# Score products on 64-row tiles in pairs, two products of the second norm on GpSimd, and another order on ScalarE

## The reference, cut to what matters

```
sa, ca, ga, sb, cb, gb = modulation(silu(c) @ wmod)     # per batch, 128 channels each
h = layernorm(x) * (1 + ca) + sa
q, k, v = split(h @ w_attn);  q, k = elu(q) + 1, elu(k) + 1
S_t = S_(t-1) + k_t v_t^T;  z_t = z_(t-1) + k_t         # per head, 8 x 8 state
y_t = (q_t S_t) / (q_t . z_t + 1e-6)
x = x + ga * (y @ w_proj)
h = layernorm(x) * (1 + cb) + sb                        # the second norm
e = argmax(h @ Wg + bg)                                 # one expert per token
x = x + gb * (gelu(h @ W1[e]) @ W2[e])
```

## Time and profile before

| | us |
|---|---|
| median of three runs | 343.55 |
| lowest and highest | 339.87, 344.41 |
| span of the profiled execution | 339.4 |
| stretch of the first 7 steps (about) | 30 to 207 |
| one full step | 24.70 |
| last step, then the tail of routing | 207 to 252 |
| experts | 252 to 339 |

### The profile page before, as it was taken

The page is one execution under the profiler, slowest core; times in us unless marked ns, Lnnn a source line. Parts: engine busy times, 40 slices in busy tenths (PEclk is TensorE's granted clock), DMA queues, the critical chain, the costliest instruction groups (busy, mean ns, idle before and its releaser), DMA issues.

```text
span 339.4 us, 10754 instructions
## 1 busy us (share of the span) xinstructions
PE 285.0 (84%) x3847; PEld 245.5 (72%) x3847; DVE 241.9 (71%) x842; ACT 152.0 (45%) x301; POOL 124.8 (37%) x142
## 2 busy tenths in 40 slices
PE   1777989999999999999999998942129999999980
PEld 1446678688688788787787887742119999999980
DVE  4974557778778778778687787663735888988880
ACT  3378491780871871861952830000023444444430
POOL 8979000303503404305305205232311546545662
PEclk9997999999999999999999999785558999999995
DMA  7990000001000001001001001000252334333410
GB/s 212 319 302 5 3 2 2 2 3 35 34 4 37 27 0 48 16 0 63 1 0 64 0 0 66 2 34 33 82 162 70 108 90 117 93 95 97 113 38 0
DMA packets 16906, 20.19 MB, mean 59 GB/s; under 512 B 2747, under 2 KB 13117, under 8 KB 16882
## 3 DMA queue, kind: packets, MB, share of 16 engines
q1 hardware_dynamic: 13040, 12.50, 13.1%
q0 software_dynamic: 2832, 6.57, 5.6%
q10 hardware_dynamic: 1010, 0.81, 0.8%
HBM read 12.22 MB, written 8.10 MB: 60 GB/s over the span
## 4 chain that ended last, share of the span: by engine, by line
PE 63%; DVE 15%; issue 6%; ACT 4%; POOL 3%; DMA 3%; DVEq 2%; SPq 1%; POOLq 0%; ACTq 0%
PE bank L1001 18%; PE bank L1013 5%; PE bank L1138 5%; PE bank L1147 4%; PE bank L1033 4%; PE bank L1020 4%; PE bank L956 3%; DVE k_q L885 3%; PE bank L1062 3%; PE bank L979 2%; PE bank L971 2%; ACT h_t L432 2%; POOL sorted_rows L374 2%; PE bank L962 2%; PE bank L1047 2%
## 5 line engine op out<-in xcount | busy, mean ns | idle before, releaser
L374 POOL DMA_INDIRECT sorted_rows<-row_buf,slot_i x32 | 31.6, 987 | 119.7 <-DVE slot_i L777 112.4
L1001 PE MATMUL bank<-q_m,k_q 128*64 128x128 f32 x1024 | 71.9, 284 | 2.6 <-DVE probs L654 2.0
L654 DVE TENSOR_TENSOR probs<-bank,causal 128x256 f32<-128x256 f32 x128 | 51.6, 421 | 22.8 <-PE bank L1001 21.9
L1001 PEld LDWEIGHTS bank<-q_m,k_q 128*64 128x64 f32 x1024 | 56.2, 140 | 10.5 <-DVE probs L654 5.9
L396 POOL DMA_INDIRECT out_dram<-q_m,slot_token x39 | 40.8, 1047 | 44.9 <-DVE q_m L901 27.1
L1138 PE MATMUL bank<-q_m,k_q 128*128 128x128 f32 x312 | 43.0, 283 | 0.0
L1147 PE MATMUL bank<-k_q,v_m 128*128 128x128 f32 x312 | 41.5, 276 | 0.0
L1138 PEld LDWEIGHTS bank<-q_m,k_q 128*128 128x128 f32 x312 | 39.6, 199 | 0.0
L1147 PEld LDWEIGHTS bank<-k_q,v_m 128*128 128x128 f32 x312 | 38.1, 193 | 0.4 <-DVE q_m L898 0.4
L541 ACT ACTIVATE v_m<-bank 128x512 f32<-128x512 f32 x39 | 23.3, 598 | 27.2 <-PE bank L1138 27.2
L484 ACT ACTIVATE rden<-bank 128x512 f32<-128x512 f32 x8 | 4.8, 597 | 49.7 <-PE bank L987 49.6
(11 more groups left out here) (177 smaller groups left out, 510.6 us busy)
## 6 DMA issues: line engine op xcount, KB each, us to landing
v_m<-sorted_rows SPq DMA_DIRECT2D x39, 132.0 KB, 2.1
x_all<-in_L_attn_x_dram SPq DMA_DIRECT2D x16, 128.0 KB, 4.2
w_all<-in_L_ffn_W_dram SPq DMA_DIRECT2D x1, 2048.0 KB, 9.6
out_dram<-q_m,slot_token POOLq DMA_INDIRECT x39, 2.3
sorted_rows<-zeros ACTq DMA_DIRECT2D x4, 132.0 KB, 2.3
sorted_rows<-zeros SPq DMA_DIRECT2D x4, 132.0 KB, 2.5
sorted_rows<-row_buf,slot_i POOLq DMA_INDIRECT x32, 2.4
wmod_sb<-in_L_wmod_dram SPq DMA_DIRECT2D x1, 384.0 KB, 4.8
```

The costliest lines, as they stand in the source:

```text
L374: pool.indirect_dma_start(sorted_rows, bass.IndirectOffsetOnAxis(ap=slot_i[par][:, t:t + 1], axis=0), row_buf[par][:, t, :], None).then_in ...
L654: V.tensor_tensor(probs[:, s, b, q, :], score_bank[q % 2][:, 0:QUADS * L], causal[:].rearrange("p a t -> p (a t)"), ALU.mult).then_inc(pro ...
L1001: last = mm(score_bank[q % 2][L * half:L * half + L, 2 * L * n:2 * L * n + 2 * L], k_q[par][:, q, tok:tok + L], q_m[par][:, 2 * half:2 * h ...
```

## The change

`core_scores` now takes two quarters at once. FIRST is (0, 2) and LAST is (1, 3), and `ORDER` gives the new order of quarters. Quarters 0 and 1 live on rows 0 to 63 and go to bank S0, quarters 2 and 3 on rows 64 to 127 and go to S1 (`score_bank[q // 2]`). Each product reads only the 64 rows that hold its quarter; the very first product of a call reads only its 32. The two quarters alternate product by product. One wait, ahead of the call, asks for all quarters before it to be out of their banks. The number of products and of columns is the same.

On POOL, `route_norm` does the product with 1 + cb and the sum with sb as well, each behind a wait for the step before it; `route_modulate` on DVE stays for the last group alone. On ACT, `route_turned` comes before `front_norm`.

```diff
-FIRST, LAST = (0, 1), (2, 3)
+FIRST, LAST = (0, 2), (1, 3)
+ORDER = FIRST + LAST
...
                                         ).then_inc(plain_ready, 1)
+                by_batch = h2.rearrange("p (b s) c -> p b s c", b=B)
+                pool.wait_ge(gates_ready, 1)
+                pool.wait_ge(plain_ready, ready)
+                nc.gpsimd.tensor_tensor(by_batch, by_batch, mod_bc[:, :, 2, :].unsqueeze(2).broadcast_to([P, B, 2, C]),
+                                        ALU.mult).then_inc(scaled, 1)
+                pool.wait_ge(gates_ready, 1)
+                pool.wait_ge(scaled, ready)
+                nc.gpsimd.tensor_tensor(by_batch, by_batch, mod_bc[:, :, 1, :].unsqueeze(2).broadcast_to([P, B, 2, C]),
+                                        ALU.add).then_inc(h2_ready, 1)
...
                     front_kn(f, fpar)
+                if route:
+                    route_turned(g - 1)
                 if norm:
                     front_norm(f + 1)
-                if route:
-                    route_turned(g - 1)
...
                 for q in quads:
-                    dve.wait_ge(score_mm, 16 * g + 8 * s + 4 * b + q + 1)
-                    V.tensor_tensor(probs[:, s, b, q, :], score_bank[q % 2][:, 0:QUADS * L],
+                    dve.wait_ge(score_mm, 16 * g + 8 * s + 4 * b + ORDER.index(q) + 1)
+                    V.tensor_tensor(probs[:, s, b, q, :], score_bank[q // 2][:, 0:QUADS * L],
...
-                if route:
-                    route_modulate(g - 1, 1 - par, chain)
...
-                for q in quads:
-
-                    pe.wait_ge(probs_ready, 16 * g + 8 * s + 4 * b + q + 1)
-                    for n in range(2):
-                        tok = t * P + n * L
-                        for half in range(2):
-                            last = mm(score_bank[q % 2][L * half:L * half + L, 2 * L * n:2 * L * n + 2 * L],
-                                      k_q[par][:, q, tok:tok + L], q_m[par][:, 2 * half:2 * half + 2, tok:tok + L],
-                                      start=True, stop=True)
-                    last.then_inc(score_mm, 1)
+                pe.wait_ge(probs_ready, 16 * g + 8 * s + 4 * b + ORDER.index(quads[1]) + 1)
+                for n in range(2):
+                    tok = t * P + n * L
+                    for half in range(2):
+                        for q in quads:
+                            rows = slice(L * (q // 2), L * (q // 2) + L)
+                            if n == half == 0 and q == quads[0]:
+                                rows = slice(32 * q, 32 * q + 32)
+                            last = mm(score_bank[q // 2][L * half:L * half + L, 2 * L * n:2 * L * n + 2 * L],
+                                      k_q[par][rows, q, tok:tok + L],
+                                      q_m[par][rows, 2 * half:2 * half + 2, tok:tok + L], start=True, stop=True)
+                            if n == 1 and half == 1:
+                                last.then_inc(score_mm, 1)
...
-            core_scores(0, 0, 0, 0)
+            core_scores(0, 0, 0, 0, FIRST)
+            core_scores(0, 0, 0, 0, LAST)
```

More of the change, by code:

```diff
@@ L210, in build @@
         proj_mm, x1_ready = sem("proj_mm"), sem("x1_ready")
-        var2_ready, guess2_ready, norm2_ready, centred, plain_ready = (
-            sem(n) for n in ("var2_ready", "guess2_ready", "norm2_ready", "centred", "plain_ready"))
+        var2_ready, guess2_ready, norm2_ready, centred, plain_ready, scaled = (
+            sem(n) for n in ("var2_ready", "guess2_ready", "norm2_ready", "centred", "plain_ready", "scaled"))
         h2_ready, h2t_mm, h2t_ready, logit_mm, onehot_ready, rank_mm, slots_ready = (
@@ L648, in first_z_and_rden, with core_probs @@
                 rden_and_slots(0, 0, 0, chain, True, False)
-            def core_probs(g, s, b, quads=range(QUADS)):
+            def core_probs(g, s, b, quads=ORDER):
                 wait_ge(dve, y_mm, 4 * g + 2 * s - 1)
                 for q in quads:
-                    dve.wait_ge(score_mm, 16 * g + 8 * s + 4 * b + q + 1)
-                    V.tensor_tensor(probs[:, s, b, q, :], score_bank[q % 2][:, 0:QUADS * L],
+                    dve.wait_ge(score_mm, 16 * g + 8 * s + 4 * b + ORDER.index(q) + 1)
+                    V.tensor_tensor(probs[:, s, b, q, :], score_bank[q // 2][:, 0:QUADS * L],
                                     causal[:].rearrange("p a t -> p (a t)"), ALU.mult).then_inc(probs_ready, 1)
@@ L699, in route_newton, with route_modulate @@
                 newton(rstd2[:], guess2[:], newton2[:], var2[:], chain).then_inc(norm2_ready, 1)
[L701 to L708, removed]
+            def route_modulate(r, par, chain):
+                for t in range(GT):
+                    last = V.tensor_scalar(row_buf[par][:, t, 0:C], row_buf[par][:, t, C:2 * C],
+                                           mean2[:, t:t + 1], rstd2[:, t:t + 1], ALU.subtract, ALU.mult)
+                chain.link(last)
                 h2 = row_buf[par][:, :, 0:C].rearrange("p (b s) c -> p b s c", b=B)
@@ L777, in rden_and_slots @@
                     V.tensor_copy(slot_i[par][:], slot_f[:]).then_inc(slots_ready, 1)
-            LINKS = 3 + 3 + 1 + 7 + 7
+            LINKS = 3 + 3 + 7 + 7
             def step(g, par, turn, chain, front=True, route=True):
@@ L840, in _ @@
             dve.wait_ge(norm2_ready, G)
-            route_modulate(G - 1, 1, chain, norm=True)
+            route_modulate(G - 1, 1, chain)
             z_and_argmax(G, 0, G - 1, chain, False, True)
@@ L988, in front_inv, with core_scores @@
                 last.then_inc(inv_mm, 1)
-            def core_scores(g, par, s, b, quads=range(QUADS)):
+            def core_scores(g, par, s, b, quads):
                 t = 2 * b + s
```

## The result

The changed kernel takes 397.07 us (median of four runs, 392.0 to 398.16) against 343.41 us for the kernel before: a ratio of 1.153, 95% interval 1.138 to 1.169. It is slower, as forecast, but by 53.7 us and not by 10.7, and lies far above the range of 335 to 366. The ratio compares fast runs alone, for the changed kernel the two of 396.25 and 392.0. The profiled execution is the longest of the four, 398.16 us, with a span of 396.4.

The account below looks back on a forecast made before the run. TensorE's own work was taken to bound the step (busy 24.14 of 24.70 us). Five steps +8, the step without xhat +0.6, the first +0.8, opening calls and last step +1.3 gave +10.7: 343.55 to 354 us, range 335 to 366.

Parts of the forecast that it names:

- rival D: TensorE's clock falls in part of the steps after the new waits: another 5 to 20 us, 370, chance 0.05.
- A call of 0.94: One score-product call on TensorE goes from 1.02 to 0.94 us, saving 0.08 a call.
- The lone product's part: Head of a score call: the product alone on 32 rows costs 0.22 for two records plus 0.14 for reshaping.
- the second change of shape: Within a score call, going from 32 to 64 rows costs 0.14, like the loop's changes of column width.
- Rivals A: Score calls: four tiles, first product free, call 0.58, time 335, chance 0.15; beyond 2% faster from below 0.60.
- B: Score calls: second change of shape free, lone product not, call 0.80: +3.4, 347 us, no change, chance 0.17.
- C: Score calls: row halves run one after the other, call 1.38: +34, 377 us, chance 0.08.
- The wait for both banks: Next score call waits until DVE empties both banks: 0.9 us at adjacent calls, 0.3 after the turn.
- ScalarE's order: ScalarE copies h_t before xhat, so q_m comes 4.8 after the turn; TensorE waits 0.95 in five steps.
- GpSimd's products at no cost: Two products moved from DVE to GpSimd, 1.04 each, ready before the turn: cost 0, gain 0.
- A step of 26.3: A full step of the first half, walked once round: 26.3 us, +1.6 on 24.70.
- Rival E: Waits for both banks or q_m don't matter, as freed DVE empties banks earlier: -4, 339 us, chance 0.05.

Follow-up runs that it names:

- e2: The changed kernel with full 128-row score products, no 32- or 64-row product, and ScalarE's order as before: 352.83 us, ratio 1.036.
- e1: The kernel before with score products reading only the 64 rows of their quarter, old order and waits, TensorE's loop written out: 384.53 us, ratio 1.129.
- e11: The kernel before with score products reading only the 32 rows of their quarter, old order and waits, TensorE's loop kept: 389.87 us, ratio 1.091.
- e9: The kernel before with ScalarE's new order alone, e4 again on another chip: 373.26 us, ratio 1.049.
- e10: e9 with five useless 128x128 products on TensorE where it would wait for q_m: 365.41 us, ratio 1.023.
- e4: The kernel before with ScalarE's new order alone (turned rows copied before xhat): median 367.75 us, runs 359.91 to 374.94.
- e3: The changed kernel with ScalarE's order undone (xhat again before the copy of the turned rows): 385.96 us, ratio 1.132.
- e5: The changed kernel without the lone 32-row product, ScalarE's order as before, TensorE's loop written out: 369.74 us, ratio 1.028.
- e6: The kernel before with GpSimd's two products alone, scores and ScalarE's order as before: 360.35 us, ratio 1.000.

## Why the prediction was wrong

**The step that failed is the clock (rival D).** The prediction gave it a chance of 0.05 and 5 to 20 us, and left it out of its sum of 10.7. It was in fact the main case, and with it the loss is 53.7 us: in a full step 6.1 us are lost, of which 1.7 lie in the part at full clock and 4.4 in the rest, where the prediction's own price for waits is 0.2; and up to step 1 another 13 us, of which e2, with the waits but 128 rows, has 5.4. The argument was that PE would still be busy near 90% of a step, and it was: 28.2 of 30.8. That share was the wrong thing to look at. e1 has PE busy for 137.25 of 140 us and falls to 0.83 from 60 to 200; what it changed, beside the loop written out, is only how many of the array's rows a product uses. With 32 rows and some new waits e11 falls to 0.70. Before, three quarters of the rows in each score product held zeros, and by e1 these rows counted. The Trainium skill, "TensorE: Matmul & The Clock Gate", Part 1, says that the level follows how busy TensorE has been lately; e9 against e10 (0.85 and 0.99) agrees with it, and e1 shows that busy in the profile's sense is not enough.

**The clock was also taken for granted between the calls.** I took the clock as given so long as PE was the bound. e4 and e9 show that already the one wait that I had priced for its own length alone (0.95 there, 1.26 here) lowers it, in a kernel otherwise unchanged: e9 has 1.049, and 1.023 when it is filled. e2 shows that waits of 0.64 don't in steps 1 to 6, at 128 rows; waits of 0.85 were not tried at 128 rows. So a wait for q_m and smaller tiles are each enough to lower the clock, and the changed kernel has both. How they add up isn't shown: e3, with the small tiles and the waits for probs, keeps 1.00 from 79 to 146 us, and e1, with no new wait, falls in every step.

Point by point, the rest:
- *A call of 0.94*: right, 0.95. The lone product's part was right too (0.36; e5 0.35), and so was that four tiles run side by side (0.60 in e5). That the second change of shape costs like one of column width was a guess from neighbours, and it came true: with the lone product's records alone a call would take some 0.82. Rivals A, B and C are out by this, and A's lower end is real but doesn't help: e5 isn't faster than the kernel before.
- *The wait for both banks*: right, 0.9 forecast and 0.85 measured at adjacent calls, 0.3 and 0.26 after the turn.
- *ScalarE's order*: right for the wait, 0.95 forecast and 0.97 measured, in five steps. What the wait does to the clock was left out.
- *GpSimd's products at no cost*: right in effect (e6, 1.000), though each takes 1.27 instead of the 1.04 forecast.
- *A step of 26.3*: at full clock it would be somewhat more. e3 has 25.82 without the wait for q_m; with 0.97 for it that is an estimated 26.8 (and 19.8 is measured for 19.4 of it). It is 30.8.
- *Rival E*, that the waits don't matter: out, e2 is at 1.036.

Not tried: the changed kernel with its wait for q_m filled, so that a whole step of it at full clock was never seen. Why the clock comes back, 3 to 18 us after its fall in the steps of the changed kernel and most often after some 10, is open too.

## What to carry to other kernels

Small tiles of the array save time only if TensorE keeps its clock, and full products over rows of zeros may be what keeps it: look at the granted clock per stretch, not at the busy share, and try the smaller tile alone before building on it. A wait of about a microsecond in a dense list can cost more than twice its own length: e9 lost 14 us or more to five waits of 1.26 us. Not every stop does it: in e10 two of 2.5 and 2.8 us left the clock at 1.00. When a wait is suspected, filling it with useless products is a cheap test, and here it gave back 8 of the 14 us.

## What the runs showed of the hardware

- The granted clock fell when the score products used fewer rows, with PE busy for 98% of the time from 60 to 200 us: 1.00 with 128 rows, 0.83 with 64 (e1). With 32 rows it was 0.70, PE busy for 95% (e11), on a chip where a kernel with 128 rows has 0.99 (e10).
- Five waits of 1.26 us in a kernel otherwise unchanged were each followed by a stretch at 1.2 GHz (0.85 from 60 to 200 us, e9); filled with useless products, 0.99 (e10).
- Products on four tiles of 64 rows by 64 columns run side by side: 16 records in 0.60 at full clock, against 1.02 for two tiles of 128 rows.
- A lone product on 32 rows ahead of seven on 64 costs 0.35 (0.95 against 0.60). With the estimate of 0.22 for its two records, 0.13 is left for going from 32 to 64 rows, like the 0.14 of a change of column width.
- GpSimd's product of 128 x 512 with an operand broadcast from `mod_bc` takes 1.27, with one value per row 1.04.
